# TensorE's semaphore rises moved from the last product to a drain behind it, in the first experts and the edge picks of a graph network kernel

## The chip, the cores and the metric

The kernel runs on one core of one Trainium2 chip. The metric is the device time of one execution in microseconds (us), lower is better; the times given are medians of a few runs.

## What is computed

The reference is two layers of a graph network over 3125 nodes with 256 features. Each layer adds a graph convolution and a linear attention to `x`, then a feed-forward part. The part that matters here is the feed-forward of the first layer, a mixture of four experts whose gates come from graph attention:

```python
def _L0_ffn_ref(x, W_gat, att_src, att_dst, b_gat, ln_gamma, ln_beta, W1, b1, W2, b2, edge_index):
    h = (x_flat @ W_gat).reshape(M, HEADS, NUM_EXPERTS)            # 4 heads, 4 experts
    e = leaky_relu(a_src[src] + a_dst[dst])                        # 65536 edges and a loop for each node
    alpha = softmax of e over the edges of each dst
    agg = segment_sum(h[src] * alpha, dst) + b_gat
    scores = layernorm(agg).reshape(M, HEADS, NUM_EXPERTS).mean(1)
    topk_s, topk_i = top_k(scores, 2); w = softmax(topk_s)
    for ei in range(NUM_EXPERTS):
        g = where(topk_i == ei, w, 0).sum(-1)
        hh = gelu(x @ W1[ei] + b1[ei])                             # 256 -> 512
        out = out + g * (hh @ W2[ei] + b2[ei])                     # 512 -> 256
```

(The listing is cut to what matters; the words for `alpha` and `agg` stand for several lines.)

## The kernel before, in words

The stage in question takes some 945 us out of the middle of the program (from 2103 to 3048 us of the span). Every engine has its own list of instructions, written out by hand, and they meet at semaphores. TensorE's list (the function under `@block.tensor` at L2437) does three kinds of work:

- **The experts.** Nodes are handled in G = 5 groups of 625 nodes, each of TG = 5 tiles of 125 (P). `piece_of` (L2440) makes one of 8 pieces of the hidden layer of a group: 128 hidden features by 313 or 312 nodes, the product at L2446, into PSUM bank `piece % 2`. ScalarE takes each piece out through Gelu (L2554) and raises `piece_out`. `row_of` (L2450) makes one of the 5 output tiles of the group: a product with the bias parts (L2458) and four (L2460) with `hT`, into the banks 2, 3 and 4; ScalarE copies them out (L2568) and raises `rows_out`. `expert(e, i, start, stop)` (L2464) is a loop (`pe.Fori`) over groups with 8 pieces and 5 rows in its body.
- **The picks.** `gather(b, e, i, g)` (L2480) fetches, for 128 slots of each of 128 lists of edges, 16 values of the source node out of a table held in SBUF, by products of a 0/1 matrix `src_hot` with the table (L2490). It has GPIECES = 16 pieces; each has PICKS = 3 sets ("triples", though the last has two slots) of 27, 27 and 18 products, and behind each piece one piece or row of an expert is put, so that VectorE has time to make the next 0/1 matrix (`make_hot`, L2089) and to choose from the sums (`choose`, L2103 and L2108). Two gathers run in all: the first with group 2 of expert 0, the second with group 0 of expert 1.
- **The keys.** `turn_key` (L2474) turns a tile of keys over, twice. It has one product (L2478).

TensorE tells the others that a piece, a row, a set of picks or a key is ready with `then_inc` on the last product: the semaphores `piece_done`, `rows_done`, `gathered` and `key_back`. It waits itself for `piece_out`, `rows_out`, `hot_made` and `chosen_out`. Most waits go through a helper that makes an instruction of its own of the wait (L170 and L171):

```python
def alone(eng, signal, value):
    eng.wait_ge(signal, value)
    eng.sem_inc(waits_met, 1)
```

Beside this, GpSimd fetches rows of the node table by indirect DMAs (L2327, one for each of 128 slots of a block of edges), and later the sums of each node (L2353). VectorE sums over the edges (`sum_up`), then makes the gates. TensorE turns the gates inside the fourth group of expert 3 (`turn_gates`, product L2521), and VectorE then adds up the experts' rows into `xres` (L2292 and L2300), which ends the stage.

The order of TensorE's work is fixed in the list: group 0 of expert 0, key 0, group 1, key 1, the first gather (with group 2), groups 3 and 4 of expert 0, the second gather (with group 0 of expert 1), groups 1 to 4 of expert 1, experts 2 and 3.

Of the kernel before, what the change touches and what calls it, by code (L numbers as in the profile page):

```python
# [20 lines left out]
P = N // T  # L21
# [43 lines left out]
TURNED = 128  # L65
# [13 lines left out]
def graph_kernel(nc, a, out):  # L79
    with ExitStack() as top:  # L80
# [12 lines left out]
        def keep(name, shape, dt=F32):  # L93
            return top.enter_context(nc.sbuf_tensor(name, shape, dt))
# [4 lines left out]
        ps = top.enter_context(nc.psum_tensor("ps", [128, 8, 512], F32))  # L99
# [15 lines left out]
        ident = keep("ident", [128, 128])  # L115
# [97 lines left out]
        with ExitStack() as phase:  # L213
# [12 lines left out]
            with ExitStack() as prep, nc.Block() as block:  # L226
                def q(name, shape, dt=F32):
                    return prep.enter_context(nc.sbuf_tensor(name, shape, dt))
# [16 lines left out]
                last = q("last", [128, 1])  # L245
# [1204 lines left out]
        with ExitStack() as layer:  # L1450
# [3 lines left out]
            with ExitStack() as conv:  # L1454
# [12 lines left out]
                with ExitStack() as phase, nc.Block() as block:  # L1467
# [5 lines left out]
                    w2 = s("gcn_w2", [128, 4, C])  # L1473
                    h1T = s("h1T", [128, 4, NG])
                    landed = sem("mlp0_landed")
                    piece_done = sem("mlp0_piece")
                    piece_out = sem("mlp0_piece_out")
                    rows_done = sem("mlp0_rows")
# [103 lines left out]
            with ExitStack() as mix:  # L1582
# [123 lines left out]
                with ExitStack() as phase, nc.Block() as block:  # L1706
# [14 lines left out]
                    rows_done = sem("proj0_rows")  # L1721
# [88 lines left out]
        with ExitStack() as layer:  # L1810
# [15 lines left out]
            with ExitStack() as phase, nc.Block() as block:  # L1826
# [5 lines left out]
                hT = s("gat_hT", [16, NG])  # L1832
# [4 lines left out]
                piece_done = sem("gat_piece")  # L1837
# [88 lines left out]
            with ExitStack() as routed:  # L1926
                sums_got = routed.enter_context(nc.sbuf_tensor("sums_got", [128, OWN, ACCS], F32))
                with ExitStack() as phase, nc.Block() as block:
# [39 lines left out]
                    key_f = src_f  # L1968
# [65 lines left out]
                    key_back = sem("att_key_back")  # L2034
# [4 lines left out]
                    gathered = sem("att_gathered")  # L2039
# [318 lines left out]
                    w1 = [first_w1, s("ew1_1", [128, 2, HID])]  # L2358
                    w2 = [first_w2, s("ew2_1", [128, 4, C])]
                    b1 = s("eb1", [128, EXPERTS0, 4])  # L2360
                    hT = s("ehT", [128, 4, NG])
# [4 lines left out]
                    piece_done = sem("exp0_piece")  # L2366
                    piece_out = sem("exp0_piece_out")
                    rows_done = sem("exp0_rows")
# [69 lines left out]
                    @block.tensor  # L2438
                    def _(pe):
                        def piece_of(e, i, g, piece):  # L2440

                            first, n = HALVES[piece // 4]
                            m = piece % 4
                            pe.wait_ge(piece_out, (g + e * G) * 8 + (piece + 1))
                            for c in range(2):
                                last = nc.tensor.matmul(ps[:, piece % 2, 0:n], w1[i][:, c, m * 128:(m + 1) * 128],  # L2446
                                                        xnT[:, c, ds(g * NG + first, n)], start=(c == 0), stop=(c == 1))
                            last.then_inc(piece_done, 1)

                        def row_of(e, i, g, j):  # L2450

                            run = g + e * G
                            if j == 0:
                                pe.wait_ge(piece_out, run * 8 + 10)
                                pe.wait_ge(b2_ready, 1)
                            alone(pe, rows_out, run * TG + (j + TG + 1 - Y_BACK[j]))
                            o = ps[0:P, Y_BANK[j], 0:C]
                            nc.tensor.matmul(o, parts_ones[:], b2_parts[:, e * C:(e + 1) * C], start=True, stop=False)  # L2458
                            for c in range(4):
                                last = nc.tensor.matmul(o, hT[:, c, j * P:(j + 1) * P], w2[i][:, c, :],  # L2460
                                                        start=False, stop=(c == 3))
                            last.then_inc(rows_done, 1)

                        def expert(e, i, start, stop, ahead_of_rows=None):  # L2464

                            with pe.Fori(start, stop) as g:
                                for piece in range(8):
                                    piece_of(e, i, g, piece)
                                if ahead_of_rows:
                                    ahead_of_rows()  # L2470
                                for j in range(TG):
                                    row_of(e, i, g, j)

                        def turn_key(b):  # L2474

                            alone(pe, key_ready, b + 1)
                            alone(pe, key_out, b + 1)
                            nc.tensor.transpose(ps[0:TURNED, 7, 0:128], key_f[:], ident[:]).then_inc(key_back, 1)  # L2478

                        def gather(b, e, i, g):  # L2480

                            for piece in range(GPIECES):
                                alone(pe, hot_made, b * GPIECES + piece + 1)
                                for k, (first, many) in enumerate(TRIPLES):
                                    alone(pe, chosen_out, (b * GPIECES + piece) * PICKS + k + 1)
                                    for slot in range(many):
                                        edges_of = slice((first + slot) * 128, (first + slot + 1) * 128)
                                        for tier in range(TIERS):
                                            for part in range(3):
                                                last = nc.tensor.matmul(  # L2490
                                                    pick_bank(piece % 2, k, many)[:, slot * MIDS * HROW:(slot + 1) * MIDS * HROW],
                                                    src_hot[piece % 2][0:P, tier, edges_of],
                                                    table_thirds[:, part, tier, :, :].rearrange("p c m -> p (c m)"),
                                                    start=(tier == 0 and part == 0),
                                                    stop=(tier == TIERS - 1 and part == 2))
                                    last.then_inc(gathered, 1)
                                if piece < 8:
                                    piece_of(e, i, g, piece)
                                elif piece < 8 + TG:
                                    row_of(e, i, g, piece - 8)  # L2500

                        pe.sem_inc(key_out, 1)
                        pe.sem_inc(chosen_out, 2)
                        alone(pe, w_landed[0], 32)
                        expert(0, 0, 0, 1)
                        turn_key(0)
                        expert(0, 0, 1, 2)
                        turn_key(1)
                        gather(0, 0, 0, 2)
                        expert(0, 0, 3, G)  # L2510
                        alone(pe, rows_done, T)
                        pe.sem_inc(w_used, 1)
                        alone(pe, w_landed[1], 32)
                        gather(1, 1, 1, 0)
                        expert(1, 1, 1, G)
                        alone(pe, rows_done, 2 * T)
                        pe.sem_inc(w_used, 1)
                        def turn_gates():
                            pe.wait_ge(gates_spread, 1)
                            for e in range(EXPERTS0):  # L2520
                                last = nc.tensor.matmul(ps[0:P, 7, e * T:(e + 1) * T],  # L2521
                                                        spread_gates[0:OWNERS, e, :, :].rearrange("p k d -> p (k d)"),
                                                        tile_of[0:OWNERS, :], start=True, stop=True)
                            last.then_inc(gates_turned, 1)

                        alone(pe, w_landed[0], 64)
                        expert(2, 0, 0, G)
                        alone(pe, w_landed[1], 64)
                        expert(3, 1, 0, 3)
                        expert(3, 1, 3, 4, ahead_of_rows=turn_gates)  # L2530
                        expert(3, 1, 4, G)
# [85 lines left out]
        with ExitStack() as layer:  # L2617
# [8 lines left out]
            with ExitStack() as conv:  # L2626
# [4 lines left out]
                with ExitStack() as phase, nc.Block() as block:  # L2631
# [4 lines left out]
                    w1 = s("gnn1_w1", [128, 2, C])  # L2636
                    w2 = s("gnn1_w2", [128, 2, C])
                    hT = s("gnn1_hT", [128, 2, NG])
                    landed = sem("mlp1_landed")
                    dve_step = sem("mlp1_dve")  # L2640
                    piece_done = sem("mlp1_piece")
                    piece_out = sem("mlp1_piece_out")
                    rows_done = sem("mlp1_rows")
# [78 lines left out]
            with ExitStack() as mix:  # L2722
# [647 lines left out]
                with ExitStack() as phase, nc.Block() as block:  # L3370
# [6 lines left out]
                    rows_done = sem("proj1_rows")  # L3377
# [40 lines left out]
        with ExitStack() as layer:  # L3418
# [29 lines left out]
            with ExitStack() as phase, nc.Block() as block:  # L3448
# [10 lines left out]
                piece_done = sem("router_piece")  # L3459
# [80 lines left out]
            with ExitStack() as phase, nc.Block() as block:  # L3540
# [3 lines left out]
                w1, w2, wo = ([first, s(f"{n}_1", [128, 2, C])] for n, first in zip(("f1", "f2", "fo"), f_first))  # L3544
# [5 lines left out]
                piece_done = sem("exp1_piece")  # L3550
                piece_out = sem("exp1_piece_out")
                rows_done = sem("exp1_rows")
# [133 lines left out]
```

## Time and profile before

| what | value |
|---|---|
| median of 3 runs | 4632.89 us (4626.37 to 4638.28) |
| the profiled execution | 4626.74 us |
| its span in the trace | 4624.8 us |
| TensorE busy | 3742.1 us, 81% of the span |
| VectorE, ScalarE, GpSimd busy | 48%, 29%, 15% |
| mean granted TensorE clock | 0.886 of full speed |

The profiled execution's own time is 1.9 us more than its span, which is what lies before the first and behind the last instruction that the trace has. A row of a trace view names the line, the engine, the operation, the tile written and those read. "PE" is TensorE's products, "PEld" its weight loads, "PEldq" what TensorE's sequencer does itself (drains, waits, registers, branches), DVE is VectorE, ACT ScalarE, POOL GpSimd. Matmul ends are modelled, so a group of them is best read by its start and the start of the next.

### The profile page before, as it was taken

What the parts mean: (1) busy time and instruction counts of PE and PEld (TensorE: products, weight loads), DVE (VectorE), ACT (ScalarE), POOL (GpSimd) and SP (SyncE); (2) the same over time, 40 slices, a digit from 0 to 9 for tenths busy, and PEclk for the clock granted to TensorE, in tenths of its full rate; (3) what the DMA queues carried; (4) which work ended last, traced back from release to release, by engine and by line L of the source; (5) the groups of instructions that cost most, each with busy time, mean ns of one, the idle gap of its engine ahead of it and who ended that gap; (6) DMA issues with size and microseconds to landing.
All of it is one profiled execution on the core that took longest, in us unless ns stands there. A gap on an engine that the chain in (4) does not pass through costs nothing. (4 is left out here: it accounts for less than half of the span.)

```text
span 4624.8 us, 91402 instructions
## 1 busy us (share of the span) xinstructions
PE 3742.1 (81%) x23942; PEld 2677.0 (58%) x23943; DVE 2236.7 (48%) x5781; ACT 1346.1 (29%) x2980; POOL 672.0 (15%) x1160
## 2 busy tenths in 40 slices
PE   4888865799789989985193677959989899799998
PEld 2444433566478669753082555649879444457776
DVE  7888878888810121143072455160220777623333
ACT  2555532677710110231010022330000135233333
POOL 3222100000000000014605222000000466100000
PEclk9999975778799899997596788979999999889999
DMA  2111220222134115202111131224335100100000
GB/s 105 47 72 75 91 93 0 84 89 91 71 141 170 56 71 202 82 14 54 14 49 33 18 33 56 95 98 180 129 112 207 35 1 1 16 18 7 14 14 28
DMA packets 124630, 319.58 MB, mean 69 GB/s; under 512 B 42658, under 2 KB 74897, under 8 KB 109228
## 3 DMA queue, kind: packets, MB, share of 16 engines
q1 hardware_dynamic: 111332, 302.42, 18.7%
q0 software_dynamic: 9760, 8.89, 1.9%
q10 hardware_dynamic: 3404, 6.53, 0.4%
q8 instruction: 78, 1.28, 0.1%
q14 instruction: 56, 0.46, 0.0%
HBM read 245.52 MB, written 72.43 MB: 69 GB/s over the span
## 5 line engine op out<-in xcount | busy, mean ns | idle before, releaser
L557 PE MATMUL ps<-hot_key,hot_src 128*126 128x512 bf16 (+1 forms) x2208 | 416.9, 314 | 39.7 <-DVE hot_key L522 20.8
L522 DVE TENSOR_SCALAR hot_key<-col_iota,run_keys 128x625 bf16<-128x625 int16 x1104 | 394.0, 379 | 0.0
L1338 PE MATMUL ps<-gnn_u_thirds,near 125*128 125x256 bf16 x3000 | 337.2, 275 | 22.3 <-issue 22.3
L557 PEld LDWEIGHTS ps<-hot_key,hot_src 128*126 128x126 bf16 x2208 | 212.7, 136 | 235.4 <-DVE hot_key L522 172.5
L1338 PEld LDWEIGHTS ps<-gnn_u_thirds,near 125*128 125x128 bf16 x3000 | 331.1, 141 | 27.1 <-issue 24.3
L2490 PE MATMUL ps<-table_thirds,rows_room 125*128 125x144 bf16 x2304 | 173.7, 232 | 199.1 <-issue 181.0
L2490 PEld LDWEIGHTS ps<-table_thirds,rows_room 125*128 125x128 bf16 x2304 | 154.4, 100 | 221.7 <-issue 219.1
L2446 PE MATMUL ps<-xnT,ew 128*128 (+2 forms) x640 | 206.5, 475 | 80.0 <-issue 48.5
L519 DVE TENSOR_SCALAR hot_src<-col_iota,run_srcs 128x125 bf16<-128x125 int16 x828 | 211.8, 256 | 98.4 <-PE ps L557 49.6
L866 PE MATMUL ps<-row_hot,slot_hot 128*128 128x512 f16 x1088 | 223.7, 359 | 1.5 <-DVE row_hot L1079 1.0
L3640 DVE SCALAR_TENSOR_TENSOR xres<-ps,shares,xres 125x256 f32 x200 | 96.8, 484 | 241.7 <-PE ps L3605 220.8
L2446 PEld LDWEIGHTS ps<-xnT,ew 128*128 128x128 f32 x640 | 128.6, 209 | 145.5 <-issue 75.3
L2460 PE MATMUL ps<-ew,ehT 128*125 128x256 f32 x800 | 208.7, 406 | 0.0
L2103 DVE TENSOR_TENSOR gat_chosen<-ps,last_rows 128x432 f32<-128x432 f32 (+1 forms) x96 | 53.4, 556 | 317.3 <-remote 223.2
L2554 ACT ACTIVATE ehT<-ps,eb 128x313 f32<-128x313 f32 (+1 forms) x160 | 82.6, 521 | 405.1 <-PE ps L2446 217.7
L3594 PE MATMUL ps<-xnT,f 128*128 x640 | 185.4, 437 | 12.2 <-ACTq L3613 4.6
L1079 DVE TENSOR_SCALAR row_hot<-row_iota,row_of 128x670 f16<-128x670 int16 x544 | 189.7, 391 | 0.3 <-issue 0.3
L1338 PE MATMUL ps<-agg_u_thirds,near 125*128 125x257 bf16 x1500 | 174.8, 277 | 10.4 <-issue 9.9
L3594 PE MATMUL ps<-f_h1T,f 128*128 128x313 f32 (+1 forms) x640 | 180.1, 434 | 0.0
L3605 PE MATMUL ps<-fo,f_h2T 128*125 128x256 f32 x800 | 179.2, 379 | 0.0
L1338 PEld LDWEIGHTS ps<-agg_u_thirds,near 125*128 125x128 bf16 x1500 | 169.3, 141 | 16.4 <-issue 15.6
L1338 PE MATMUL ps<-gcn_u_thirds,near 125*128 125x256 bf16 x1500 | 167.2, 275 | 12.7 <-DVEq L1557 12.7
(570 smaller groups left out, 6853.9 us busy)
## 6 DMA issues: line engine op xcount, KB each, us to landing
near<-adjacency SPq DMA_DIRECT2D x80, 1562.5 KB, 6.5
adjacency<-counts SPq DMA_DIRECT2D x125, 312.5 KB, 2.2
own_in<-own_rows SPq DMA_DIRECT2D x34, 512.0 KB, 4.0
expert_rows<-rows_y SPq DMA_DIRECT2D x75, 125.0 KB
rows_room<-expert_rows SPq DMA_DIRECT2D x25, 375.0 KB
pair_in<-high_rows SPq DMA_DIRECT2D x34, 256.0 KB, 4.8
pair_in<-low_rows SPq DMA_DIRECT2D x34, 256.0 KB, 5.3
rows_room<-key_rows SPq DMA_DIRECT2D x8, 1024.0 KB
```

The lines of the kernel that those rows point to most:

```text
L519: nc.vector.tensor_scalar(hot_src[:, j, 0:P], col_iota[:, 0:P], run_srcs[:, ds(at, 1), j:j + 1].rearrange("p a j -> p (a j)"), None, ALU.i ...
L522: nc.vector.tensor_scalar(hot_key[:, j, :], col_iota[:], run_keys[:, ds(at, 1), j:j + 1].rearrange("p a j -> p (a j)"), None, ALU.is_equal ...
L557: last = nc.tensor.matmul(sums[:, b:e], hot_src[:, j, :], hot_key[:, j, b:e], start=False, stop=True, skip_group_check=True)
L866: last = nc.tensor.matmul(ps[:, bank, 0:e - b], slot_hot[:, c % RING, :], row_hot[:, c % RING, b:e], start=False, stop=True, skip_group_ch ...
L1079: nc.vector.tensor_scalar(row_hot[:, c % RING, :], row_iota[:], row_of[i][:, c:c + 1], None, ALU.is_equal).then_inc(routes_made, 1)
L1338: last = nc.tensor.matmul(ps[:, j, 0:width], lead_tiles[BUF[j]][:, k, :], parts.thirds[:, k, i, :], start=(k == 0 and i == 0), stop=(k == ...
L2446: last = nc.tensor.matmul(ps[:, piece % 2, 0:n], w1[i][:, c, m * 128:(m + 1) * 128], xnT[:, c, ds(g * NG + first, n)], start=(c == 0), sto ...
L2460: last = nc.tensor.matmul(o, hT[:, c, j * P:(j + 1) * P], w2[i][:, c, :], start=False, stop=(c == 3))
L2490: last = nc.tensor.matmul(pick_bank(piece % 2, k, many)[:, slot * MIDS * HROW:(slot + 1) * MIDS * HROW], src_hot[piece % 2][0:P, tier, edg ...
L3594: last = nc.tensor.matmul(ps[:, piece % 2, 0:n], (w1, w2)[stage][i][:, c, m * 128:(m + 1) * 128], moving, start=(c == 0), stop=(c == 1))
L3605: last = nc.tensor.matmul(o, h2T[:, c, j * P:(j + 1) * P], wo[i][:, c, :], start=(c == 0), stop=(c == 1))
L3640: nc.vector.scalar_tensor_tensor(x_t, ps[0:P, 2 + j, 0:C], share, x_t, ALU.mult, ALU.add).then_inc(rows_out, 1)
```

## The change

Every one of the four rises stands at a drain of TensorE behind the last product, and not at the product. A drain is an instruction of the sequencer: it is over once the engine has nothing left in flight, and the sequencer goes on to the next instruction only then. There are 160 pieces (20 groups of 8), 100 rows (20 groups of 5), 96 sets of picks (2 gathers of 16 pieces with 3) and 2 keys, so 358 drains are added to TensorE's list. The products, their order, their operands, all waits and the other engines' lists are the same as before. The rise of `turn_gates` (L2521) and all rises outside this stage stay at their products.

```diff
@@ piece_of
                             pe.wait_ge(piece_out, (g + e * G) * 8 + (piece + 1))
                             for c in range(2):
-                                last = nc.tensor.matmul(ps[:, piece % 2, 0:n], w1[i][:, c, m * 128:(m + 1) * 128],
+                                nc.tensor.matmul(ps[:, piece % 2, 0:n], w1[i][:, c, m * 128:(m + 1) * 128],
                                                         xnT[:, c, ds(g * NG + first, n)], start=(c == 0), stop=(c == 1))
-                            last.then_inc(piece_done, 1)
+                            pe.drain().then_inc(piece_done, 1)
@@ row_of
                             for c in range(4):
-                                last = nc.tensor.matmul(o, hT[:, c, j * P:(j + 1) * P], w2[i][:, c, :],
+                                nc.tensor.matmul(o, hT[:, c, j * P:(j + 1) * P], w2[i][:, c, :],
                                                         start=False, stop=(c == 3))
-                            last.then_inc(rows_done, 1)
+                            pe.drain().then_inc(rows_done, 1)
@@ turn_key
-                            nc.tensor.transpose(ps[0:TURNED, 7, 0:128], key_f[:], ident[:]).then_inc(key_back, 1)
+                            nc.tensor.transpose(ps[0:TURNED, 7, 0:128], key_f[:], ident[:])
+                            pe.drain().then_inc(key_back, 1)
@@ gather
-                                                last = nc.tensor.matmul(
+                                                nc.tensor.matmul(
                                                     pick_bank(piece % 2, k, many)[:, slot * MIDS * HROW:(slot + 1) * MIDS * HROW],
...
-                                    last.then_inc(gathered, 1)
+                                    pe.drain().then_inc(gathered, 1)
```

## Rows read from the trace of the kernel before

**Rows 1.** The page: the span, and TensorE's busy time

```profile
span 4624.8 us, 91402 instructions
PE 3742.1 (81%) x23942; PEld 2677.0 (58%) x23943; DVE 2236.7 (48%) x5781; ACT 1346.1 (29%) x2980; POOL 672.0 (15%) x1160
```

**Rows 2.** Busy time of each engine by stretches of the stage, first row the columns

```profile
core 0: us, PE busy (x) PEld busy (x) DVE busy (x) ACT busy (x) POOL busy (x), PEclk, DMA share, GB/s
...
2137.00:2214.00 77.00, 32.19 (x79) 19.83 (x78) 6.23 (x15) 5.55 (x12) 59.33 (x59) 0.65 0.23 57
2214.00:2303.00 89.00, 9.56 (x39) 3.82 (x38) 0.00 (x0) 1.43 (x4) 65.94 (x67) 0.52 0.11 14
...
2312.00:2404.00 92.00, 90.92 (x1180) 84.53 (x1181) 68.79 (x135) 6.09 (x13) 0.00 (x0) 0.98 0.14 49
2404.00:2448.00 44.00, 39.33 (x163) 27.56 (x160) 37.28 (x56) 15.39 (x29) 0.00 (x0) 1.00 0.12 36
...
2464.00:2592.00 128.00, 18.17 (x76) 7.78 (x76) 4.64 (x10) 0.52 (x1) 90.46 (x91) 0.51 0.13 9
2592.00:2676.00 84.00, 82.56 (x1078) 77.20 (x1079) 63.40 (x125) 5.57 (x12) 0.00 (x0) 0.97 0.07 22
...
2741.00:2781.00 40.00, 16.92 (x35) 8.91 (x33) 6.37 (x5) 9.38 (x15) 21.88 (x22) 0.57 0.71 17
...
2857.00:2890.00 33.00, 17.73 (x37) 8.89 (x35) 5.30 (x13) 4.45 (x9) 19.58 (x20) 0.58 0.10 14
```

**Rows 3.** The three kinds of product, by line: durations in ns, least, median, most

```profile
L2446 PE MATMUL ps<-xnT,ew x640: 423/426/890, 2103.7 to 3017.4; 128*128 x112, 128*128 128x313 f32 x24, 128*128 128x312 f32 x24
...
L2460 PE MATMUL ps<-ew,ehT x800: 379/379/790, 2124.5 to 3029.1; 128*125 128x256 f32 x160
...
L2490 PE MATMUL ps<-table_thirds,rows_room x2304: 222/226/328, 2214.3 to 2675.8; 125*128 125x144 bf16 x192
```

**Rows 4.** Instructions in order of time, PE: start us, us; picks, pieces, first rows

```profile
2671.39 4.66 PE L2490 MATMUL ps<-table_thirds,rows_room 125*128 125x144 bf16 x72 [0.25 <-DVEq L2107]
2675.88 8.63 PE L2446 MATMUL ps<-xnT,ew 128*128 x32
...
2685.62 1.99 PE L2460 MATMUL ps<-ew,ehT 128*125 128x256 f32 x8
```

**Rows 5.** The stage's last products, and the drain at the block's end (ns)

```profile
3027.51 1.99 PE L2460 MATMUL ps<-ew,ehT 128*125 128x256 f32 x8
...
L1928 PEldq DRAIN  x1: 3963/3963/3963, 3025.6 to 3025.6; - x1
```

**Rows 6.** From a rise to TensorE's next product: timeline of ACT and PE, then waits

```profile
2413.14 0.52 ACT L2554 ACTIVATE ehT<-ps,eb 128x312 f32<-128x312 f32 x1 [0.53 <-PE ps L2446]
...
2413.90 0.29 PE L2458 MATMUL ps<-eb_parts,parts_ones 3*125 3x256 bf16 x1 [0.89 <-ACT ehT L2554]
...
PE ps L2446 <- PE ps L2460: 0.8, 1, 0.8
```

**Rows 7.** What TensorE's sequencer does: waits of their own, the loop's branches (ns)

```profile
L171 PEldq EVENT_SEMAPHORE  x1404: 51/51/8450, 675.3 to 4613.7; - x176
...
L2466 PEldq COMPARE_BRANCH  x18: 67/207/219, 2133.1 to 3025.5; - x18
```

**Rows 8.** Timeline inside the slow stretch from 2214 us: PE, PEld, ACT

```profile
2242.03 0.28 PE L2490 MATMUL ps<-table_thirds,rows_room 125*128 125x144 bf16 x1 [1.81 <-issue]
...
2243.43 0.10 PEld L2490 LDWEIGHTS ps<-table_thirds,rows_room 125*128 125x128 bf16 x1 [2.69 <-issue]
...
2260.34 0.38 ACT L2568 ACTIVATE rows_y<-ps 125x256 f32<-125x256 f32 x1 [24.82 <-remote]
```

**Rows 9.** TensorE's waits ahead of the second gather

```profile
PE ps L2490 <- DVE rows_room L2089: 8.1, 1, 8.1
```

**Rows 10.** The last work of the stage on VectorE

```profile
3046.31 1.73 DVE L2305 BATCH_NORM_STATS2 norm_stats<-xres 125x6 f32<-125x256 f32 x5
```

**Rows 11.** Busy time in an earlier stage with gaps between short runs of products

```profile
462.00:578.00 116.00, 95.53 (x498) 49.98 (x499) 95.47 (x382) 69.11 (x175) 23.25 (x109) 1.00 0.23 90
```

## The prediction

> **What bounds the kernel now.** I read first the page: TensorE is busy for 3742 of 4625 us [rows 1], but no other engine is over half, and the stage in question decides by stretches. So next came the busy time by stretches [rows 2]. Two kinds alternate. In the *full* stretches TensorE has nearly no idle time: 90.9 of 92 us in the first gather from 2312 on, 82.6 of 84 in the second, and in the experts' groups 18 to 19 of every 20 us. What a drain adds to TensorE there is added to the stage. In the *slow* stretches, each with GpSimd issuing its indirect DMAs (59, 67, 91, 22 and 14 operations of POOL in them), TensorE is idle for 44.8, 79.4, 109.8, 23.1 and 15.3 us (length less busy), 272 us together.
>
> The timeline shows what the slow stretches are [rows 8]: products and weight loads begin 1.40 us apart (2242.03, then 2243.43), with "issue" as the reason, inside a set of 27 products that holds no wait and no rise. ScalarE waits 24.8 us for a row there, about 18 instructions at 1.40 us. So the products are started thinly, and their rises come late on top of it. It ends when GpSimd's work ends, not when TensorE has done some amount.
>
> The stage's end: TensorE's last product ends at 3029.5 [rows 5], VectorE's last operation at 3048 [rows 10]. VectorE's chain hangs on the gates that TensorE turns before the last 13 pieces and rows. Those 13 drains lie under a slack of 18.5 us and cost nothing; with a smaller slack than their 7 us they would.
>
> **The price of one drain.** Three terms.
> 1. The tail. Products overlap: 32 of the pieces' take 8.63 us [rows 4], (8.63 - 0.43) / 31 = 0.265 us apart, while one lasts 0.426 [rows 3]. The part that the next one covers, 0.16 us, is laid bare. For the rows' products it is 0.379 - (1.99 - 0.38) / 7 = 0.15, for the picks' 0.226 - (4.66 - 0.23) / 71 = 0.16.
> 2. The drain itself. The one drain in the trace at a block's end starts at 3025.6, lasts 3.963 us and so ends at 3029.56, 0.06 us behind the modelled end of the last product at 3029.50 [rows 5]. I take 0.05.
> 3. The restart. Until now the sequencer ran ahead; behind a drain the next wait, weight load and product start from nothing. Nearest row: ScalarE ends at 2413.66 and the product that waited for it starts at 2413.90 [rows 6], 0.24 us.
>
> Sum 0.45 us. Below: the tail alone, 0.16, if the next instructions are fetched and checked during the drain. Above: TensorE's wait for a product of its own takes 0.84 us [rows 6], with the tail 1.0. I take 0.45, since the 0.84 holds several waits and register steps of the sequencer, at 0.05 us each [rows 7], and most places in the program have one or two.
>
> **The sum, place by place.**
> - *A group of 8 pieces and 5 rows.* Seven pieces and four rows at 0.45 make 4.95. The eighth piece stands ahead of a wait for ScalarE of 0.89 us [rows 6], which covers all but 0.05. The fifth row stands ahead of the loop's end: 0.45, and the branch of 0.21 us [rows 7] with its register steps, hidden behind queued products until now, together some 0.5 more. 6.0 us per group.
> - *First gather.* 16 x 72 picks' products with 8 pieces (4 each) and 5 rows (9 each) are 1229; 1180 are in the full stretch [rows 2]. The 49 before it are two sets. So 61 - 2 = 59 drains at 0.45: 26.5 us. VectorE is 75% busy there (68.8 of 92) and does not become the bound, since TensorE only gets slower.
> - *Expert 0, groups 3 and 4.* 12.0 us, but TensorE then waits 8.1 us for VectorE ahead of the second gather [rows 9]; that cover is used up first: 3.9.
> - *Second gather.* 1078 of 1229 products are in the full stretch; the 151 before it are six sets and two pieces. 53 drains: 23.9.
> - *Expert 1, four groups:* 24.0. *Expert 2, five:* 30.0. *Expert 3, three groups and 8 pieces up to the gates:* 18 + 3.3 = 21.3.
> - *Two keys, and group 0 and 1 of expert 0:* ahead of or in the slow stretch whose end GpSimd sets. Nothing; without that cover some 12 us more.
> - *Slow stretches.* Taken at no change. They end with GpSimd. A gain would be rises that come sooner, at most the two short ones' idle time (38 us) and some of the refilling behind the long ones (17), so -55; a loss is some 10 us, if each drain lets the queue run empty.
> - The other engines' small stalls that now overlap: -2.
>
> 26.5 + 3.9 + 23.9 + 24 + 30 + 21.3 = 129.6, less 2: +128 us. On the profiled execution's 4626.7 us that is 4755; the median stands 6 above that execution, so **4761 us**. At 0.16 a drain, with the same steps, the sum is about 50 (4683); at 1.0 about 280 (4913).
>
> **The rivals.** A measurement of this kernel can tell about 0.3% from no change, 14 us.
>
> *A, the forecast (65%).* As summed.
>
> *B, the drain's rise is not late (14%).* In the slow stretches a rise may be late because a product's completion is reported late. If the drain is over when the array is empty, without those reports, ScalarE and VectorE get their work in time, and the 55 us above come back: 4761 - 55 = 4706. For it: ScalarE's wait of 24.8 us is far longer than a product takes [rows 8]. Against: a drain must know that all is done, and nothing in the trace shows that it has a quicker way to know than the rises have. [...]
>
> *C, the clock falls (6%).* With a gap of 0.3 us or so behind each piece, TensorE's granted clock could drop from 1.00 to half in the full stretches. Products then last twice as long (890 ns against 426 is the most in the rows [rows 3]): some 19 us in each of the 14 groups behind the slow stretches, +266, and up to +174 with the gathers: 5020 to 5200. Against: in an earlier stretch TensorE is busy for 95.5 of 116 us, in short runs with gaps, at a clock of 1.00 [rows 11], and with the drains its share would be about the same, 20 of 26. [...]
>
> *D, nearly free (4%).* If the drain waits only for instructions to be handed over, it costs its 0.05 us: 358 x 0.05 = 18, most of it beside other work: 4640. Against: the drain of 3.96 us, which ended with the products [rows 5].
>
> *E, faster (11%).* The slow stretches may come from products in flight: the sequencer is far ahead with up to some 50 instructions whose completions it waits for, at one per 1.40 us. If a drain clears that backlog at once, TensorE does in these stretches the work that now waits behind them. The place is the gathers and groups beside GpSimd's DMAs, the price up to the 272 us of idle time [rows 2]: 4761 - 272 = 4489. It decides from 128 of 272, that is when 47% of the idle time goes. For it: the exact 1.40 us inside a set looks like a wait for something handed out one at a time. Against: the same step holds for weight loads and products that raise nothing, and it ends when GpSimd stops, so that it looks like a rate that GpSimd's work leaves, and a drain does not raise a rate.
>
> **How the numbers follow.** The time is A's. A's bounds are 4683 and 4913, with most of it between 4700 and 4850; B at 4706 lies within. Low 4685, high 4870 leaves out C, D and E (21% together) but for E's mild cases, and A's far upper end. Faster by over 0.3%: E with its larger effects, 0.10. Within 0.3%: D, and E with half of the idle time gone, 0.05. Slower: A, B and C, 0.85.
>
> **What would show it.** In the profile after, TensorE's sequencer has 358 more drains in four lines. Starts of pieces in a group move from 1.06 to about 1.5 us apart, a group from about 20.2 to 26. In the gathers the step from the last product of a set to the next set's first is about 0.4 us longer. The first gather's full stretch grows by 26, the stage by about 128, with the granted clock at 1.00 in the full stretches. The slow stretches keep their lengths and their 1.40 us, TensorE's wait of 8.1 us for VectorE is gone, and VectorE still ends the stage, some 11 us behind TensorE. Wrong: slow stretches shorter than before, or products closer than 1.40 us in them (E); ScalarE's long waits gone at unchanged steps (B); a clock under 0.9 in the experts (C); pieces still 1.06 us apart (D).

## The result and the profile after

The changed kernel takes 4750.73 us (median of 4 runs, 4747.1 to 4755.36), the kernel before 4635.59 us beside it: 1.0248 times as long, with a 95% interval of 1.0229 to 1.0267. That is 115 us slower. The forecast was 4761 us, 128 us more than the 4633 known then, in a range from 4685 to 4870.

The page of the profiled execution, to be laid beside [rows 1]. The span grew by 120.3 us, TensorE's busy time by only 28: most of the added time is idle time of TensorE.

```profile
span 4745.1 us, 91710 instructions
PE 3769.7 (79%) x23892; PEld 2672.0 (56%) x23943; DVE 2237.2 (47%) x5781; ACT 1346.7 (28%) x2980; POOL 674.5 (14%) x1160
```

The added drains, by line: durations in ns (least, median, most), first and last start. All 358 are there.

```profile
L2448 PEldq DRAIN  x160: 1123/1312/6967, 2103.6 to 3143.4; - x160
L2462 PEldq DRAIN  x100: 2030/2188/25032, 2125.5 to 3155.4; - x100
L2497 PEldq DRAIN  x96: 303/1288/73518, 2296.5 to 2735.3; - x96
L2479 PEldq DRAIN  x2: 277/1852/3427, 2139.9 to 2291.7; - x2
```

No drain ended before the recorded end of its last product, 20 ns behind it at the least, and no product or weight load started sooner than 52 ns after a drain was over. A median drain is as long as the products that it was put behind and costs little of that itself. What it costs is read from the starts of the products. Here is the timeline of PE inside the third group of expert 1:

```profile
2763.09 1.32 PE L2446 MATMUL ps<-xnT,ew 128*128 x4 [0.71 <-issue]
2764.62 1.32 PE L2446 MATMUL ps<-xnT,ew 128*128 x4 [0.22 <-issue]
2766.15 1.32 PE L2446 MATMUL ps<-xnT,ew 128*128 x4 [0.21 <-issue]
2767.68 1.32 PE L2446 MATMUL ps<-xnT,ew 128*128 x4 [0.21 <-issue]
...
2781.84 0.29 PE L2458 MATMUL ps<-eb_parts,parts_ones 3*125 3x256 bf16 x1 [0.32 <-issue]
2782.06 1.99 PE L2460 MATMUL ps<-ew,ehT 128*125 128x256 f32 x8
2784.38 0.29 PE L2458 MATMUL ps<-eb_parts,parts_ones 3*125 3x256 bf16 x1 [0.32 <-issue]
```

A piece comes every 1.53 us, where 32 products in a row gave 1.06 in [rows 4]: 0.48 more. A row comes every 2.54, against 2.17 before: 0.36 more. The 0.48 can be taken apart: 0.16 is the bared tail, 0.21 the gap between the last product's end and the next one's start (0.02 until the drain is over, 0.19 until the next weight load), and 0.10 the first product itself, which lasts 0.526 us behind a drain instead of 0.426. Its weight load starts only 0.01 us ahead of it, where it used to lie beside an earlier product; that this is the reason is likely, but no run shows it.

In the second gather the three sets of a piece, 27, 27 and 18 products, used to run as 72 in one go, 4.66 us. Now (timeline of PE, with the piece before and behind):

```profile
2639.65 1.32 PE L2446 MATMUL ps<-xnT,ew 128*128 128x313 f32 x4
2641.34 1.85 PE L2491 MATMUL ps<-table_thirds,rows_room 125*128 125x144 bf16 x27 [0.38 <-issue]
2643.43 1.85 PE L2491 MATMUL ps<-table_thirds,rows_room 125*128 125x144 bf16 x27 [0.23 <-issue]
2645.51 1.28 PE L2491 MATMUL ps<-table_thirds,rows_room 125*128 125x144 bf16 x18 [0.23 <-issue]
2646.87 1.32 PE L2446 MATMUL ps<-xnT,ew 128*128 128x313 f32 x4
```

The sets take 5.53 us from 2641.34 to 2646.87, where it was 4.50: 0.34 for each. The piece with its two waits takes 1.69 instead of 1.10.

**The slow stretches look different, and are as long as before.** TensorE's products in the second of them, from the timeline of PE, and the drain behind the second line's set:

```profile
2517.49 2.45 PE L2446 MATMUL ps<-xnT,ew 128*128 128x313 f32 x4 [11.79 <-issue]
2524.86 3.40 PE L2491 MATMUL ps<-table_thirds,rows_room 125*128 125x144 bf16 x27 [4.92 <-issue]
2599.64 3.40 PE L2491 MATMUL ps<-table_thirds,rows_room 125*128 125x144 bf16 x27 [71.38 <-issue]
```

```profile
L2497 PEldq DRAIN  x1: 73518/73518/73518, 2525.9 to 2525.9; - x1
```

The set's 27 products are started within 3.4 us, close together, and then the drain lasts 73.5 us. 27 products with their weight loads are 54 instructions: 1.36 us each. In another place a row's 18 instructions have a drain of 25.0 us, 1.39 each. Before, the starts lay 1.40 us apart [rows 8]; now what lies so far apart is the reported end. So the products are not started slowly: TensorE's completions come slowly. In the kernel before, 63 products and weight loads had been started behind a row's last product when ScalarE took the row (three rows in turn, at 2235.14, 2260.34 and 2284.84 us; the prediction had some 50), and the starts came at the rate of the completions. Here all 54 were started within 3.4 us, and the last was complete some 71 us later. The recorded end of a product, which is modelled, is no measure of this: in the kernel before, ScalarE took a row 0.13 us behind the recorded end of its last product in the median, and 70.9 us behind it at the most, in these stretches. GpSimd's fetches, whose end ends these stretches, show the length: in the first line of L2327 after, the starts span 169.5 us, and in the kernel before they span 168.8. The 96 fetches of the second line up to their first pause take 124.7 us in both kernels.

```profile
L2327 POOL DMA_INDIRECT rows_room<-node_table,src_idx x128: 996/996/1720, 2134.2 to 2303.7; - x128
L2327 POOL DMA_INDIRECT last_rows<-node_table,src_idx x128: 996/1000/1917, 2493.2 to 2837.3; - x128
```

Busy time by stretches, for [rows 2] (PE, PEld, DVE, ACT, POOL, then the granted clock, the DMA share and GB/s): the first gather's full stretch, groups 3 and 4 of expert 0, the second slow stretch, the second gather, and expert 3 up to the gates.

```profile
2321.00:2433.00 112.00, 96.51 (x1158) 80.75 (x1158) 68.11 (x133) 6.10 (x13) 0.00 (x0) 1.00 0.13 44
2433.00:2485.00 52.00, 42.31 (x145) 25.30 (x145) 37.14 (x56) 15.03 (x28) 0.00 (x0) 0.97 0.07 22
2490.00:2630.00 140.00, 19.30 (x144) 16.84 (x145) 9.88 (x20) 0.52 (x1) 98.34 (x98) 0.53 0.18 26
2630.00:2737.00 107.00, 92.34 (x1089) 76.96 (x1087) 63.53 (x124) 5.58 (x12) 0.00 (x0) 0.98 0.05 17
...
3029.00:3119.00 90.00, 74.58 (x262) 44.72 (x263) 10.01 (x36) 27.52 (x53) 0.00 (x0) 1.00 0.28 108
```

The granted clock in the full stretches stays at 0.97 to 1.00, with TensorE busy for 81 to 86% of them; in the gathers it was 98 to 99% before. What does grow is the time that TensorE takes to get going again when the fetches end. From the end of the first block's last fetch to the third set of the first gather it is 11.1 us before and 14.1 after, and from the end of the 96th fetch of the second block to the second set of the second gather's second piece 14.1 and 18.3. In the three experiments whose kernels have no drains up to there, the first is 11.1 to 13.2 us and the second 14.3 to 15.5.

TensorE's last row starts at 3155.38, 128.1 us later than before. VectorE's last operation of the stage, against [rows 10], is 123.5 us later: its chain covers the 4.6 us of the drains behind the gates. They are 18, not the 13 of the prediction, which left out the five rows of the fourth group. In the rest of the program 3.2 us come back.

```profile
3169.77 1.73 DVE L2305 BATCH_NORM_STATS2 norm_stats<-xres 125x6 f32<-125x256 f32 x5
```

### The profile page after: what moved, and what is told of

Same layout as the page of the kernel before. It is cut to its first block and busy times, and to the rows that moved or that the text cites. A ratio compares the mean times of both kernels' runs of the same rounds, so it can differ in the third digit from the quotient of the medians.

```text
span 4745.1 us, 91710 instructions
## 1 busy us (share of the span) xinstructions
PE 3769.7 (79%) x23892; PEld 2672.0 (56%) x23943; DVE 2237.2 (47%) x5781; ACT 1346.7 (28%) x2980; POOL 674.5 (14%) x1160
## 3 DMA queue, kind: packets, MB, share of 16 engines
q1 hardware_dynamic: 111332, 302.42, 18.3%
## 5 line engine op out<-in xcount | busy, mean ns | idle before, releaser
L2446 PE MATMUL ps<-xnT,ew 128*128 (+2 forms) x640 | 226.4, 479 | 99.8 <-issue 72.9
L2446 PEld LDWEIGHTS ps<-xnT,ew 128*128 128x128 f32 x640 | 115.8, 201 | 202.0 <-issue 151.5
```

## The experiments

Two theories. *The price is local*: each drain costs TensorE its bared tail and a restart, 0.3 to 0.5 us where nothing covers it, whatever its rise is for. *The price is the rise or the reports*: the others get their work late, or the drains wait for the late completions of the slow stretches.

### One kind of drain at a time

The edit for the pieces; rows and picks alone have it in the same way at their places.

```diff
-                            last.then_inc(piece_done, 1)
+                            pe.drain().then_inc(piece_done, 1)
```

> Drains behind the 160 pieces alone. Theory (each drain costs where it stands, by bared tail and restart): in the changed kernel's trace the seven steps between a group's pieces grew by 0.49 us each on average, 3.46, the eighth by 0.12, so 3.6 us in each of 14 groups, 50, and 0.59 us behind each of 14 gather pieces, 8; a few us are covered. +55 us on the kernel before. Rival (the whole cost is one effect that any drain brings on, for instance that TensorE's queue never runs ahead any more): well over half of the 115 us, 80 or more, and the three partial kernels add up to far more than the whole.

> Drains behind the 100 rows alone. Theory: four rows at 0.37 us and the last one, ahead of the loop's end, at 0.84 us, 2.3 us in each of 14 groups, 32, and 10 gather rows at 0.5, 5: +36 us. Rival as for the pieces: 80 or more.

> Drains behind the 96 sets of picks alone. Theory: three sets took 4.50 us before and 5.52 with drains, 0.34 for each of some 90 sets in the full stretches: +31 us. With the pieces' 55 and the rows' 36 the sum is 122, near the whole change's 120 in the profiled executions. Rival: VectorE, which makes the next 0/1 matrix and chooses from the sums, gets its work later and adds to it: over 45.

Measured, all on one chip with the kernel before at 4633.01: pieces 4680.01 (+47.0, ratio 1.0102, interval 1.0085 to 1.0119), rows 4658.96 (+26.0; 1.006, 1.0044 to 1.0077), picks 4668.04 (+35.0; 1.0077, 1.006 to 1.0094). Together 108 us of 115, which is no difference at intervals of some 8 us each: the kinds add up, and no kind brings the others' cost with it. A full group takes 20.2 us before, 23.8 with the pieces' drains, 22.6 with the rows', 26.15 with both: 3.6 and 2.4 make 6.0. Pieces and rows came out 8 and 10 us under what their steps promised, because a group in which TensorE waits for something else gives part of it back: with the pieces' drains alone the last group before the gates grows by 0.3 us instead of 3.6.

### The rise back at the product

```diff
                             last.then_inc(piece_done, 1)
+                            pe.drain()
```

> The 358 drains stand where the change has them, but the rise is back at the last product. Theory (the drain holds up what is behind it on TensorE, and the place of the rise is worth nothing, since a product's rise and the drain's lie some 0.05 us apart): as the changed kernel, +110 to +120 us on the kernel before. Rival (the others get their work late because the rise is late): clearly less, below +80.

4744.62 us, +111.6 (1.0237, 1.0219 to 1.0254), against the changed kernel's 1.0248, inside its interval. A group takes 25.9 to 26.0 us instead of 26.15. The cost is that the sequencer stands still, not that ScalarE and VectorE hear of it later. The rival falls.

### An instruction without a drain, and a second drain

The first edit is made on the kernel before, the second on the changed one, each in all four places.

```diff
                             last.then_inc(piece_done, 1)
+                            pe.sem_inc(waits_met, 1)
```

```diff
+                            pe.drain()
                             pe.drain().then_inc(piece_done, 1)
```

> The kernel before with one more semaphore instruction of the sequencer in each of the 358 places, and no drain. Theory (the cost is the emptying of the array, not one more instruction): the sequencer runs ahead of the products and the 51 ns lie beside them, 0 to +3 us. Rival (an instruction of the sequencer's own costs its time wherever it stands): 358 x 0.05 to 0.1, +18 to +36.

> Two drains in each of the 358 places. Theory: the second one finds the array empty and costs only the sequencer's step, 0.05 to 0.1 us for each of some 300 that are not covered: +15 to +30 on the changed kernel, so +130 to +145 on the kernel before. Rival (a drain has a fixed price of its own of 0.3 us or more): +90 and more on the changed kernel.

The semaphore instruction: 4632.55 us against 4633.31, ratio 1.0002 (0.9992 to 1.0012). It takes 51 ns each and costs nothing. The pieces still come as they did (timeline of PE):

```profile
2679.45 8.63 PE L2446 MATMUL ps<-xnT,ew 128*128 x32
```

Two drains: 4776.64 us, +143.3 (1.0312, 1.0295 to 1.033), some 28 us more than the changed kernel, where +15 to +30 was expected and the rival wanted 90. The second drain of each piece, by its line:

```profile
L2449 PEldq DRAIN  x160: 13/13/141, 2109.2 to 3177.5; - x160
```

It lasts 13 ns, and a group grows from 26.15 to 27.3 us, 0.09 us for each of the 13: an exposed step of the sequencer, and no fixed price of a drain. An instruction of the sequencer's own that does no work on the array cost 0.00 us here beside products (the semaphore instruction) and 0.09 behind a drain (the second drain).

### The loops written out

```diff
-                            with pe.Fori(start, stop) as g:
+                            for g in range(start, stop):
```

> The changed kernel with TensorE's loops over the groups written out, so that no register step and no branch stands between a drain and the next weight load. In the changed kernel's trace the pieces of a group whose loop has one turn come 1.39 us apart and those in a loop 1.53, rows 2.44 against 2.53. Theory (part of the restart is the sequencer's register steps, bare behind a drain): 13 groups x (7 x 0.14 + 5 x 0.09 + 0.5 for the branch), 1.9 us each, 25 us less than the changed kernel, so +90 on the kernel before. Rival (the restart is the array's own): as the changed kernel, +115.

> The kernel before with the same loops written out, no drains. Theory (the register steps lie beside queued products there): 0 to -5 us, since the loop's end is hidden too. Rival (the steps cost something before as well): -20 us or more, and then part of what is put down to the drains is not theirs.

With drains 4733.92 us, +100.6 (1.0214, 1.0197 to 1.0231), some 15 us less than the changed kernel's +115; 25 were expected. Its rows come 2.44 us apart everywhere (timeline of PE):

```profile
3036.46 1.99 PE L2460 MATMUL ps<-ew,ehT 128*125 128x256 f32 x8
3038.68 0.29 PE L2458 MATMUL ps<-eb_parts,parts_ones 3*125 3x256 bf16 x1 [0.23 <-issue]
3038.90 1.99 PE L2460 MATMUL ps<-ew,ehT 128*125 128x256 f32 x8
```

A full group takes 23.9 us instead of 26.15. So 2.2 of the 6.0 us are register steps and the branch of the loop, bare behind a drain. 13 groups of it would be 28 us. The starts of the groups in the two traces show where the rest stays: only six run full in both and give 2.0 to 2.3 each, and a seventh, with a short wait, gives 1.5. Of the others, the last before the gates lasts 25.4 in both, group 4 of expert 0 grows from 33.2 to 34.0, and those that lie beside GpSimd's indirect DMAs give 1 us in sum. Without drains the same edit gives 4628.35 against 4633.31, ratio 0.9987 (0.9978 to 0.9997): 5 us, and a group of 20.1 instead of 20.2. Of the kernels here that compute the reference it is the fastest, if by a tenth of a per cent.

### Drains where something covers them

The first run has drains in groups 0 and 1, at the keys and in the pieces 0 and 1 of each gather (the diff shows the gather), the second only from the gates' products on (`slow[0]` becomes true there).

```diff
+                                        if slot and piece < 2:
+                                            pe.drain()
...
-                                    last.then_inc(gathered, 1)
+                                    (pe.drain() if piece < 2 else last).then_inc(gathered, 1)
```

```diff
-                            last.then_inc(piece_done, 1)
+                            (pe.drain() if slow[0] else last).then_inc(piece_done, 1)
```

> Drains only beside GpSimd's indirect DMAs: the 16 pieces and 10 rows of groups 0 and 1, the two keys, and the first two pieces of each gather, there also between the slots of a set, so three in a set of 27 products. Theory (1.40 us per instruction is a rate, and the stretch ends with GpSimd): the two long slow stretches keep their length and their 1.40 us; what comes ahead of them is covered but for the 4.9 us that the changed kernel lost up to group 2, so 0 to +8 us. Rival E of the prediction (a drain clears a backlog and the work runs on faster): tens of us faster than the kernel before.

> Drains only behind the gates' products: the last 5 rows of group 3 and the 8 pieces and 5 rows of group 4 of expert 3. Theory: TensorE's last product comes some 5 us later, under the 18.5 us by which VectorE ends behind it: within 3 us of the kernel before. Rival (VectorE's last sums wait for the rows as they come): +4 us or more.

Slack only: 4634.42 against 4633.77, ratio 1.0002 (0.9989 to 1.0015). The 18 drains cost nothing under VectorE's chain that the interval, -5 to +7 us, can tell. Slow only: 4643.75, +10.0 (1.002, 1.0008 to 1.0032), 2 us over the expected "0 to +8", and not tens of us faster. So drains beside the slow stretches are not free: in this trace too TensorE resumes late behind the fetches, 15.6 and 18.4 us where it is 11.1 to 13.2 and 14.1 to 15.5 without drains. With a drain behind every nine products the set looks like this (timeline of PE):

```profile
2539.42 1.26 PE L2496 MATMUL ps<-table_thirds,rows_room 125*128 125x144 bf16 x9 [23.69 <-issue]
2564.63 1.26 PE L2496 MATMUL ps<-table_thirds,rows_room 125*128 125x144 bf16 x9 [23.95 <-issue]
2589.99 1.24 PE L2496 MATMUL ps<-table_thirds,rows_room 125*128 125x144 bf16 x9 [24.11 <-issue]
```

Nine products with their loads, 18 instructions, every 25.2 to 25.4 us: again 1.40 each, in whatever portions they are sent. It is a rate of completions, and a drain neither clears nor speeds it. That settles rival E of the prediction.

### GpSimd's fetches without an index

```diff
-                                pool.indirect_dma_start(
-                                    out=fetched[q][:, j, :], out_offset=None, in_=node_table,
-                                    in_offset=bass.IndirectOffsetOnAxis(ap=src_idx[:, q, j:j + 1], axis=0),
-                                    bounds_check=N - 1, oob_is_err=False).then_inc(got[q], 16)
+                                pool.dma_start(out=fetched[q][:, j, :], in_=node_table[0:128, :]).then_inc(got[q], 16)
```

> No drains; GpSimd's 128 indirect DMAs for each block of edges are plain ones of the same size that read the first 128 rows of the node table, so the fetched rows are not those of the edges and the sums are others. Theory: the slow start of products, 1.40 us apart, comes with GpSimd's writing of indirect transfers; with plain ones TensorE's instructions go at full speed or the stretch is shorter, 50 us and more are gained. Rival (it has to do with the transfers' traffic, or with the waits around them): TensorE's 1.40 us stay, the time is within 30 us of the kernel before.

4318.93 us against 4633.77 on the same chip: ratio 0.932 (0.9301 to 0.9339), 315 us less. The two stretches in which GpSimd fetches (columns as above):

```profile
2124.00:2206.00 82.00, 81.20 (x808) 68.80 (x807) 50.25 (x109) 12.65 (x28) 72.31 (x130) 0.99 0.38 103
...
2297.00:2352.00 55.00, 52.81 (x688) 49.33 (x689) 43.05 (x85) 4.18 (x8) 54.35 (x98) 0.97 0.36 88
```

TensorE is busy for 81.2 of 82 and 52.8 of 55 us beside them, where it had 9.56 of 89 and 18.17 of 128 [rows 2]. Each fetch is of the same size and takes GpSimd 0.76 us in the first block and 0.59 in the second (medians) instead of 1.0, and all queues together move 103 and 88 GB/s beside them, where it was 14 and 9. So it is not GpSimd's work or its traffic as such: on this chip TensorE's completions are slow beside the *indirect* DMAs. The same run bears it out, since the 25 indirect DMAs with which GpSimd later fetches the sums of each node are still in it. Beside them the slow stretch stays, and the group of expert 2 beside them takes 44.1 us (before: 44.7):

```profile
2542.00:2575.00 33.00, 14.62 (x58) 10.16 (x57) 0.00 (x0) 2.96 (x7) 25.05 (x25) 0.76 0.17 27
```

How much of the 315 us comes from that, and how much from fetches that are themselves over sooner, one run does not tell.

> The changed kernel with GpSimd's indirect DMAs for the edges replaced by plain ones as in the run without drains, which took 4318.9 us (again the fetched rows are not those of the edges). Theory (the price of a drain is TensorE's own, and slow stretches only cover some of it): the 115 us of the change and the drains of the groups and sets that lay beside the slow stretches, some 20 at 0.4 us: 4319 + 115 to 130, 4434 to 4449. No drain lasts longer than a few us. Rival (much of the 115 us comes from drains that wait in slow stretches for late completions): 4319 + 90 or less.

4428.75 us, 5 under the expected range. This run was on another chip, and there the kernel before took 4302.36 us (7 runs, 4298.96 to 4305.51), 331 less than the medians of 4633 to 4636 in all other comparisons. The ratio on that chip is 1.0297 (1.028 to 1.0315), +126 us for both edits together; against the run without drains, on the other chip, it is +110. Both are near the +115 to +130 that the local price asks for, and over the rival's 90. But the +126 also contains what the plain fetches do on that chip, and the +110 compares two chips. The 96 picks' drains are short now:

```profile
L2494 PEldq DRAIN  x96: 753/1288/2368, 2168.6 to 2462.2; - x96
```

No trace of the kernel before was taken on that chip, but this trace shows what indirect DMAs do there. The same 25 of them, 1.0 us each, are still in it, beside two groups of expert 2:

```profile
2639.00:2672.00 33.00, 26.97 (x99) 16.54 (x98) 0.00 (x0) 7.51 (x16) 24.98 (x25) 1.00 0.16 27
...
L2350 POOL DMA_INDIRECT sums_got<-edge_sums,end_i x25: 992/997/1044, 2639.4 to 2670.7; - x25
```

In 33 us with as many operations of GpSimd and the same 27 GB/s, TensorE is busy for 27.0 us here and for 14.6 on the other chip. The two groups beside them take 26.15 and 26.14 us, as every full group with drains does, and no drain in them lasts over 2.2 us. In the changed kernel's own trace the 25 fall into one group, and it takes 46.6. So the slow completions beside indirect DMAs are there on the chip of the other run and not on this one, which fits the 4302 us of the kernel before. Whether that is the chip or a state that it was in, what makes the completions slow, and whether the plain fetches gain anything here, stays open. The numbers of this document on drains in full stretches do not hang on it.

## Why the prediction was right

The sum, place by place, read from the starts of the same product before and after:

| place | forecast, us | measured, us |
|---|---|---|
| up to the first gather's full stretch | 0 | 4.9 |
| first gather | 26.5 | 23.7 |
| expert 0, groups 3 and 4, up to the second gather's full stretch | 3.9 | 12.5 |
| second gather | 23.9 | 20.0 |
| expert 1 | 24.0 | 20.2 |
| expert 2 | 30.0 | 25.9 |
| expert 3 up to the gates | 21.3 | 16.2 |
| sum | 129.6 | 123.4 |

The total came out closer than its terms, and that is luck, since misses cancel: two places cost 13.5 us more than forecast and five cost 19.7 less. The table is also one pair of executions. Expert 1 alone took 117.5 us in the trace before and 119.5 to 127.4 in five experiments without drains in it, against 137.8 after, so its 20.2 may be 10 as well; the stretch ahead of the first gather took 210.2 before, 211.4 to 212.9 in three experiments without drains, and 215.2 after. The medians lie 115 us apart, the profiled executions 120.

- **The price of one drain** was 0.45 us; it is 0.48 for a piece and 0.36 for a row in a loop, 0.34 for a piece and 0.27 for a row outside one, 0.34 for a set of picks. The tail of 0.16 was right. The drain's own time is 0.02, not 0.05: in the median it ends 0.02 us behind the modelled end of its last product. The restart of 0.24 was right by luck: from the drain's end to the next weight load it is 0.19 for a piece in a loop, and the 0.10 by which the first product is longer had no term in the sum. The restart depends on how many sequencer steps stand behind the drain, as the runs with written-out loops (a row every 2.44 us instead of 2.54) and two drains (0.09 us for the second) show. In the full stretches of the gathers 46 and 42 of the drains are those of sets, at 0.34, while their pieces cost 0.59 and their rows 0.5, with two waits behind them; that is why the two gathers came out 3 and 4 us under.
- **A group** was 6.0 us and is 5.9 where it runs full. The experts still fell 13 us short of their 75.3. In groups with a wait of TensorE for ScalarE, the drains lie in that wait: one group of expert 1 grew only from 25.0 to 29.3, and the last before the gates from 24.0 to 25.4. The term "small stalls, -2" was the mis-sized one.
- **The wait of 8.1 us for VectorE** [rows 9] was to swallow most of 12 us. That step failed. The wait only shrank to 4.6, since VectorE was later too: its sums wait for ScalarE's exponentials, which stand in ScalarE's list among the pieces of group 4. The waits of DVE after (before, the same wait took 4.46 us):

```profile
DVE rows_room L2161 <- ACT rows_room L2540: 12.9, 1, 12.9
```

  So the next block's fetches began 36.0 us later, at 2493.2 for 2457.2, while the first gather's end had moved by 28.6. A cover is only one if what makes it does not itself hang on the engine that is slowed.
- **Slow stretches at no change** holds but for some 10 us: GpSimd's fetches take as long as before, and 17 drains of more than 5 us each, 326 us in all, cost little of that. The 4.9 us ahead of the first gather's full stretch and 5.1 of the 12.5 ahead of the second's are lost by the time these stretches end, and the run with drains beside the slow stretches alone gives +10.0. It is the loss that the prediction named, some 10 us if each drain lets the queue run empty, and left out of the sum. What I said one would see there was wrong: the starts are not 1.40 us apart any more, though the rate is the same. Read from starts alone, as in [rows 8], late completions, with 63 instructions started ahead of them, look like slow issue.
- **Rival B** is out: the drain of 73.5 us ends some 71 us behind the modelled end of its last product, so it is held with the completions. The rise comes with the drain's end: ScalarE started on a piece or a row never less than 0.12 us after its drain was over, 0.13 in the median, and the drain is over late.
- **Rival C** is out: the granted clock is 0.97 to 1.00 in the full stretches with a gap behind each piece. In the third group of expert 1, where TensorE waits for ScalarE, the clock is 0.94, and before it was 0.93.
- **D** is out by the second gather's 0.34 us a set, **E** by the run with drains beside the slow stretches alone. The sign that was to speak for E, products closer than 1.40 us in a slow stretch, did appear, and it did not mean E: the drains end at the old rate.

## What to carry to other kernels

In this kernel a drain of TensorE between short runs of products cost the overlap of two products (0.16 us) plus every step of its sequencer up to the next one, 0.3 to 0.5 us together; leave the rise at the product, or, where a drain must be, keep register steps and waits away from behind it. Count such a cost only where its engine has no slack, and before you let a wait swallow it, follow that wait back to see that it does not move along. If TensorE's instructions start evenly and far apart, as at 1.40 us here, look at what another engine does at the same time before you blame the list.

## What was not expected of the hardware

- Beside GpSimd's indirect DMAs (1.0 us each, one every 1.3 us) TensorE's completions come one per 1.36 to 1.40 us, weight loads and products alike, with 54 instructions started and not yet complete in the changed kernel and 63 in the one before; beside plain DMAs of the same size TensorE is busy for 81.2 of 82 us. Between the two kernels lie 315 us on the chip where both were run.
- That slowness is not on every chip: beside the same 25 indirect DMAs a group takes 44.1 us without drains on one chip, and on another the two groups there take 26.1 each with drains. The kernel before takes 4633 to 4636 us (medians) in all comparisons but the last, and 4302 on the chip of the last.
- A drain on an empty TensorE takes 13 ns, and 0.09 us with its step.
